# GpSimd's order in one tile of a mixture-of-experts layer: output indices ahead of a gather, a scatter for each block of tokens

## The reference, cut to what matters

```python
x = x + conv_attention(layernorm_over_channels(x))     # x: (2, 256, 32, 32) float32
t = to_tokens(x)                                       # 2048 tokens x 256
xt = layernorm_over_tokens(t)
gate = softmax(xt @ Wg); topv, topi = top_k(gate, 2)   # 8 experts, 2 for each token
topv = topv / (sum(topv) + 1e-6)
scores = zeros(2048, 8); scores[token, topi] = topv
out = 0
for e in range(8):
    h = gelu(xt @ W1[e] + b1[e])                       # 256 -> 1024
    out = out + (h @ W2[e] + b2[e]) * scores[:, e:e+1] # 1024 -> 256
t = t + out
```

## Time and profile before

| | us |
|---|---|
| time, median of 3 runs (lowest, highest) | 436.52 (436.09, 436.82) |
| the profiled execution: its own time | 437.19 |
| the profiled execution: span | 435.4 |
| TensorE busy (share of the span) | 373.3 (86%) |
| VectorE busy | 267.0 (61%) |
| ScalarE busy | 248.1 (57%) |
| GpSimd busy | 185.5 (43%) |
| chain that ended last: TensorE, issue, GpSimd, DMA | 35%, 8%, 8%, 4% of the span |

### The profile page before, as it was taken

The page is one execution under the profiler, slowest core; times in us unless marked ns, Lnnn a source line. Parts: engine busy times, 40 slices in busy tenths (PEclk is TensorE's granted clock), DMA queues, the critical chain, the costliest instruction groups (busy, mean ns, idle before and its releaser), DMA issues.

```text
span 435.4 us, 8097 instructions
## 1 busy us (share of the span) xinstructions
PE 373.3 (86%) x2476; PEld 334.5 (77%) x2476; DVE 267.0 (61%) x684; ACT 248.1 (57%) x522; POOL 185.5 (43%) x279
## 2 busy tenths in 40 slices
PE   5889969989998657899999999799997999899960
PEld 4435557877787646899989998799987998799960
DVE  4668478796898995275447447584365754734430
ACT  1386557647516752385567467486575846655530
POOL 4610000003056565316656557535565265636553
PEclk9699999999996555799999999899999999989995
DMA  8710000000020754708324733648326434322332
GB/s 273 226 36 2 0 1 2 0 2 1 2 96 2 293 169 139 250 6 254 63 53 78 205 58 62 184 98 237 63 52 178 92 54 64 53 41 52 49 53 32
DMA packets 22983, 38.91 MB, mean 89 GB/s; under 512 B 2576, under 2 KB 17296, under 8 KB 22800
## 3 DMA queue, kind: packets, MB, share of 16 engines
q1 hardware_dynamic: 14896, 25.41, 17.3%
q0 software_dynamic: 8032, 12.82, 17.1%
HBM read 28.85 MB, written 9.37 MB: 88 GB/s over the span
## 4 chain that ended last, share of the span: by engine, by line
PE 35%; issue 8%; POOL 8%; DMA 4%; DVE 1%; POOLq 1%; DVEq 1%; ACT 0%; ACTq 0%
POOL xg L533 7%; PE banks L1538 6%; PE banks L1237 6%; PE banks L1238 5%; PE banks L1239 5%; PE banks L1540 5%; PE banks L1542 5%; PE banks L1515 3%; DMA xg<-xn_rows,idx_in 3%; DMA out_rows<-y_out,idx_out 1%; DVE h_lo L1187 1%; PE banks L1571 1%; DVE y_out L1211 1%; POOL out_rows L579 0%; POOL idx_out L571 0%
## 5 line engine op out<-in xcount | busy, mean ns | idle before, releaser
L802 ACT ACTIVATE h_raw<-banks,b1t 128x256 f32<-128x256 f32 (+1 forms) x136 | 67.2, 494 | 88.0 <-PE banks L1239 87.3
L1187 DVE TENSOR_TENSOR h_lo<-h_raw,h_hi 128x256 fp32r<-128x256 f32 (+1 forms) x136 | 58.8, 443 | 68.0 <-ACT h_hi L805 67.0
L1538 PE MATMUL banks<-w_hi,h_hi 128*128 128x256 f32 x288 | 83.8, 291 | 5.7 <-DVE h_lo L1187 5.6
L1237 PE MATMUL banks<-x_hi,w_hi 128*128 128x256 f32 (+1 forms) x272 | 81.0, 298 | 8.3 <-issue 8.3
L1540 PE MATMUL banks<-w_lo,h_hi 128*128 128x256 f32 x288 | 81.3, 282 | 0.0
L1542 PE MATMUL banks<-w_hi,h_lo 128*128 128x256 f32 x288 | 81.3, 282 | 0.0
L1238 PE MATMUL banks<-x_lo,w_hi 128*128 128x256 f32 (+1 forms) x272 | 79.9, 294 | 0.9 <-issue 0.9
L1239 PE MATMUL banks<-x_hi,w_lo 128*128 128x256 f32 (+1 forms) x272 | 79.9, 294 | 0.0
L579 POOL DMA_INDIRECT out_rows<-y_out,idx_out x36 | 61.4, 1705 | 33.7 <-DVE y_out L1211 27.9
L533 POOL DMA_INDIRECT xg<-xn_rows,idx_in x57 | 56.4, 990 | 28.0 <-POOL idx_in L528 15.4
L805 ACT ACTIVATE h_hi<-banks,b1t 128x256 fp32r<-128x256 f32 (+1 forms) x136 | 66.9, 492 | 0.0
(11 more groups left out here) (217 smaller groups left out, 686.4 us busy)
## 6 DMA issues: line engine op xcount, KB each, us to landing
w_raw<-in_w SPq DMA_DIRECT2D x16, 1024.0 KB, 7.8
xn_rows<-xn SPq DMA_DIRECT2D x2, 1056.0 KB, 4.7
x<-in_x_tok SPq DMA_DIRECT2D x4, 512.0 KB, 5.8
out_rows<-x SPq DMA_DIRECT2D x1, 2048.0 KB, 9.3
b2b<-in_b SPq DMA_DIRECT2D x1, 1024.0 KB, 4.4
xg<-xn_rows,idx_in POOLq DMA_INDIRECT x57
out_rows<-y_out,idx_out POOLq DMA_INDIRECT x36, 3.9
out_rows<-x POOLq DMA_DIRECT2D x1, 384.0 KB, 3.2
```

The costliest lines, as they stand in the source:

```text
L802: act.activation(h_raw[j % RING][:, 0:w], banks[:, j % RING, 0:w], ACT.Gelu, bias=bias)
L1187: dve.tensor_tensor(h_lo[:, j, 0:w], h_raw[j % RING][:, 0:w], h_hi[:, j, 0:w].bitcast(F32), ALU.subtract).then_inc(h_split, 1)
L1237: pe.matmul(out, a_hi, b_hi, start=start, stop=False)
L1538: pe.matmul(out, h_hi[:, j, r], w_hi[e % 2][:, c], start=j == 0 and i < 2, stop=False, skip_group_check=width == WIDE)
```

## The change

On GpSimd the wait for y_added, the copy of the output indices and the signal y_free go ahead of the gather of tile t+2 (but stay behind `keep_scores`). The single wait for y_out becomes a wait ahead of each block's scatter; each is on a semaphore that VectorE now raises for each block and no longer for each tile, so both engines count in blocks. For that VectorE needs the number of odd experts before each expert: it loads eight more values into registers (`wides`) ahead of its first tile, behind the eight that it loads already.

```diff
--- before.py
+++ after.py
@@ GpSimd, tile(t, e, block, width)
                 pool.wait_ge(scores_moved, t + 1)
                 keep_scores(t + 1)
-                pool.wait_ge(scores_kept, t + 2)
-                pool.wait_ge(xg_turned, t + 2)
-                gather(t + 2)
-
-
                 pool.wait_ge(y_added, block * 16 + 16)
                 pool.tensor_copy(idx_out[:, :], row_out[:, bass.ds(t, 1), :].rearrange("p a w -> p (a w)")
                                  ).then_inc(idx_out_set, 1)
                 pool.wait_ge(idx_out_set, t + 1)
                 pool.sem_inc(y_free, 1)
 
-                pool.wait_ge(y_weighted, t + 2)
-                pool.sem_inc(adds_begun, 1)
+                pool.wait_ge(scores_kept, t + 2)
+                pool.wait_ge(xg_turned, t + 2)
+                gather(t + 2)
+
                 for i in range(width):
+
+                    pool.wait_ge(y_weighted, block + i + 2)
+                    pool.sem_inc(adds_begun, 1)
                     pool.indirect_dma_start(out_d, bass.IndirectOffsetOnAxis(ap=idx_out[:, i:i + 1], axis=0),
                                             y_out[:, i, :], None, compute_op=ALU.add).then_inc(y_added, 16)
                 move_scores(t + 1)
@@ VectorE
             experts = [expert_bounds(dve, e) for e in range(E)]
+            wides = [dve.value_load(bounds[0:1, 1, e:e + 1], min_val=0, max_val=E) for e in range(E)]
...
-                dve.wait_ge(y_weighted, t + 1)
+                dve.wait_ge(y_weighted, block + 1)
...
                 for i in range(width):
-                    ins = dve.tensor_scalar(y_out[:, i, :], y_sum[:, i, :], score[:, i, e:e + 1], None, ALU.mult)
-                ins.then_inc(y_weighted, 1)
+                    dve.tensor_scalar(y_out[:, i, :], y_sum[:, i, :], score[:, i, e:e + 1], None, ALU.mult
+                                      ).then_inc(y_weighted, 1)
```

More of the change, by code:

```diff
@@ L1180, in x_low, with tile @@
                                   ALU.subtract).then_inc(x_split, 1)
-            def tile(t, e, width, split):
+            def tile(t, e, block, width, split):
                 w = width * P
@@ L1217, in _ @@
             dve.sem_inc(y_weighted, 1)
-            t0 = 0
+            t0, odd0 = 0, 0
             x_low(0)
@@ L1222, in _ @@
                 t1, odd, more = experts[e]
+                odd1 = wides[e]
                 with dve.If(odd):
-                    tile(t0, e, WIDE, True)
+                    tile(t0, e, t0 * 2 + odd0, WIDE, True)
                 with dve.Else():
-                    tile(t0, e, 2, True)
+                    tile(t0, e, t0 * 2 + odd0, 2, True)
                 with dve.If(more):
                     with dve.Fori(t0 + 1, t1) as t:
-                        tile(t, e, 2, False)
+                        tile(t, e, t * 2 + odd1, 2, False)
                 t0 = t1
+                odd0 = odd1
         @block.tensor
```

## The result

The changed kernel took 444.09 us (median of 4 runs, 442.79 to 448.69), the one before 436.67 beside it. The ratio is 1.0176 (interval 1.0105 to 1.0247), slower by more than the noise, where 431.0 us was forecast. The profiled execution took 448.69, the longest of the four, with a span of 446.9 against 435.4; it shows more of the loss than the others have. Ratios here leave out slow runs (by the granted clock, or over 1.5% above the kernel's fastest) and medians don't, so the two can differ by up to 0.7%, and kernels are compared by their ratios.

A forecast was written before the change was run, and what follows sets the result against it. TensorE, busy 86% of the span, was taken as the bound. -2.4 - 2.26 - 1.4 + 0.6 = -5.5 took 437.19 to 431.7, or 431.0 us against the median; 8-in-10 range 428.8 to 434.5.

The forecast's parts named there:

- The waits: VectorE's 21.4 us wait for y_free falls near 0, TensorE's for h_lo from 5.6 to under 1; gains 2.4 and 2.26.
- the tail: After TensorE's last product: the scatter follows the third gather by 0.30, at 423.4, for -1.4 us (ends -0.6 and -1.7).
- What is late next is TensorE's own products, nothing else: Steady tile: with y_free early, TensorE finds h_lo ready, its 0.49 us wait goes, with 0.6 to spare.
- Cost 0: Gather queued behind the y_added wait, undisturbed tile: scatter lands at 231.6, before the gather's start at 234.26, so no loss.
- The register loads: VectorE's start: eight added loads at 0.59 us each, 4.7 together, delay x_lo(0) and TensorE's first product: +0.6 us.
- A scatter for each block: GpSimd's scatters: waits already met in 15 tiles, first scatter about 0.5 us sooner in the two wide ones; 0 in sum.
- The clock: TensorE's clock after gaps at experts' starts: one fall more or fewer, about 1.7 us, giving 429.3 or 432.7; no own chance.
- Rival 4: Gather behind y_added lands late beside weight loads; TensorE waits 4.0 us a time, twice: 439.0 us, chance 0.06.
- Rival 1: VectorE's y_out, now beside the third gather's issue, is held until that issue ends: 434.3 us, chance 0.12.
- Rival 2: Experts' first tiles: VectorE's wait returns as one for ScalarE, so their 2.26 us stay: 433.3 us, chance 0.08.
- Rival 3: TensorE's next h_lo is late for another reason; only the tail gains, -0.8 us with the loads: 435.7 us, chance 0.07.

The follow-up runs named there:

- e8: Changed kernel plus eight small unread GpSimd copies between gather and scatters: 436.89 us, ratio 0.9937 to the kernel before.
- e6: Kernel before, with two of the gather's three DMAs ahead of the y_added wait and y_free, the third behind: 433.14 us, ratio 0.9885.
- e2: Kernel before with only GpSimd's new order (y_added wait, output indices, y_free ahead of the gather): 439.46 us, ratio 1.0003.
- e12: Kernel before in its old order, with two more unread gather issues a tile behind the gather: 492.22 us, ratio 1.126.
- e10: Kernel before with the new order and eight small unread copies ahead of the gather, behind y_free: 439.83 us, ratio 1.0025.
- e5: Kernel before with the new order and eight small unread GpSimd copies between gather and scatters: 434.18 us, ratio 0.9949.
- e11: Kernel before with the new order and three small unread copies between gather and scatters: 433.05 us, ratio 0.9903.
- e1: The changed kernel run again, unaltered, beside the kernel before: 445.02 us, ratio 1.0119.
- e3: Kernel before, old order, with only the per-block scatter waits and their eight register loads on VectorE: 439.0 us, ratio 1.0023.
- e4: Kernel before with only the eight added register loads on VectorE, values unused: 438.03 us, ratio 0.996.
- e9: Kernel before with the gather split around y_free and per-block scatters counted in threes, without register loads: 434.95 us, ratio 0.9881.
- e14: Kernel before with the new order, whole-tile scatter and eight unused register loads on VectorE: 441.94 us, ratio 1.0114.
- e13: Kernel before with the new order and per-block scatters counted in threes, without register loads: 442.7 us, ratio 1.0129.
- e7: Changed kernel with its eight added register loads moved behind the first x_lo: 442.82 us, ratio 1.0128 to the kernel before.
- e15: Kernel before with the new order, three small copies between gather and scatters, and per-block scatters counted in threes: 433.28 us, ratio 0.9921.

## Why the prediction was wrong

*The waits.* Right in kind. VectorE's wait for y_free went; TensorE's for h_lo fell to 2.2, not below 1. Of the 13 tiles that are neither tile 1 nor one of the three, seven won 0.3 to 0.9 each and four lost 0.2 to 1.0, -2.0 in all; the tail won 1.1, where 1.4 was forecast. With the row broken, a good part of the forecast's gain is there: the change with a pause (e8) takes 0.6% less than before and e6 1.2%, where the forecast was 1.3%. But e6 splits its gather and has neither the register loads nor the scatters by block, so this is no test of the sum.

*The step that failed* is the one that ends "What is late next is TensorE's own products, nothing else", with "Cost 0" for the gather behind y_added. It asked when the gather starts and lands, and not what its new neighbour does: that the three gather issues now run into the two scatter issues. The 1.55 us of GpSimd's idle time before the scatter and the 1.60 before the gather were spent in the sum as if they were free. The order alone gave 439.5, or by its ratio of 1.0003 436.7, where the same sum without the loads makes 436.52 - 6.1 = 430.4. In its place the runs show updates of TensorE that reach ScalarE up to 3 us late: e2 and e12 that a row of five brings them, e10 against e5 that the place of the copies decides, and e5, e8 and e11 that a break between gather and scatters brings the time back. How the late updates turn into time is shown for the changed kernel only as far as the longer gaps and the lower clock.

*The register loads*, +0.6: they cost at least twice that in their own place. VectorE's eight ran 177.1 to 182.3, 0.65 apart and not 0.59, x_lo(0) began at 182.61, and TensorE stood 2.53 before its first product:

```profile
L1175 DVEq TENSOR_LOAD <-bounds x8: 297/301/311, 177.1 to 181.7; - x8
...
182.61 0.96 DVE L1180 TENSOR_TENSOR x_lo<-banks,x_hi 128x768 fp32r<-128x768 f32 x1 [10.51 <-issue]
...
183.62 0.44 PE L1241 MATMUL banks<-x_hi,w_hi 128*128 128x384 f32 x1 [2.53 <-DVE x_lo L1180]
```

Tile 1 took 1.2 to 1.3 more in e1, e3 and e4, and 2.8 more in the changed kernel's profile. Part of that is the clock with which TensorE comes into the tile, set ahead of anything in which the two kernels differ: the six products of its first turn took 1.51 us before and 0.85 in the changed kernel. Where it came in and stayed at the full clock, tile 1 took 15.5 without the loads (e5, e6, e9, e11) and 19.5 with them (changed, e14), because the wait of 2.5 is followed by a fall of the clock (0.57 in 184 to 188 of the changed kernel). Where it came in at the lower clock, tile 1 took 16.7 without the loads (before) and 17.9 with them (e3, e4, e8). In the old order this vanished from the time; in the new one the loads cost 1.1% by the ratios (e14).

*A scatter for each block*, 0: right in the old order (e3), 1.3% in the new one (e13).

*The clock* was counted as widening, one fall either way, 1.7 us. It is the largest part of the loss in the profiled execution, 5.8 us of busy time in three tiles. The forecast had no case in which the clock falls for longer at several experts' starts at once.

*The rivals.* None held. Rival 4 named the right side and the wrong place: TensorE's turns waited for the gather for 1.4 (at 251.18), not twice 4. Rival 1 fell: 21 of the 36 y_out began while GpSimd was issuing an indirect DMA, and y_out took 353 ns in the median, though the longest took 577 (346 to 356 before). Rival 2 fell with the waits of 1.01 and 0.93, which have gone from the first tiles; what is left there is below 0.3. Rival 3 falls with the tiles that are shorter.

**What stays open.** Through what the issues hold TensorE's updates is not shown: h_raw starts close behind the end of a scatter's issue in e2 (0.1), and in the middle of one in the changed kernel. Nor is the length of the row the whole condition: the kernel before has rows of three and no late update, e5 has rows of three and five late starts beside them. Nor is it shown why the gaps at the experts' starts grow. They are "issue" gaps at the branch to the next expert, longer by 0.5 to 1.9 in the changed kernel, each behind an expert's first tile in which ScalarE ran late. That TensorE's sequencer then reaches the branch with less work queued is my reading and was not tried by itself. Against it stands e5, with gaps of 3.36 and 3.46 at the first two and no late start in the tiles ahead of them.

## What to carry to other kernels

An engine's idle time between two groups of DMA issues can be what keeps other engines' semaphores on time: before closing such a gap on GpSimd, count how many indirect DMA issues would then stand in an unbroken row, and look in the trace at whether consumers still start within 0.1 us of their producer's end. Small parts that cost nothing in the old kernel (e3, e4) can cost about 1% each in the new one (e13, e14), so add parts to the old kernel and also take them from the new. Where TensorE comes out of a stretch with gaps, price the clock as a term of the sum and not as noise.

## What the runs showed of the hardware

- With five indirect DMA issues in a row on GpSimd (0.95 to 1.8 us each, 0.30 apart), TensorE's semaphore reached ScalarE up to 3.0 us late (14 to 16 starts over 1 us of 136 in the changed kernel, e1, e2, e7, e10, e13 and e14). Rows of three gave none in the kernel before, e3, e4, e6 and e9, and 5 to 11 in e5, e8, e11 and e15, where copies stand between gather and scatters.
- With a copy and 0.79 us of GpSimd's idle time inside the gather (e6) there was no late start; 1.3 us of small copies between gather and scatters (e5) left 5 of 14. Place and kind of the break differ, so which of the two matters was not told apart.
- A register load with its register operations took VectorE's sequencer 0.65 us (eight from 177.1 to 182.3).
- After gaps of 2.9 to 4.3 us in TensorE's work at three experts' starts the granted clock was 0.52 to 0.53 over 7 us.
